# One-core block of attention and mixture of experts: the eight experts over all tokens, or over tokens sorted into tiles by expert

## What is computed

```python
h = _layernorm(x) * (1 + ca) + sa
x = x + ga * attention(h)
h = _layernorm(x) * (1 + cb) + sb
logits = h @ router_w.T
top_w, top_idx = top_k(softmax(logits), 2)
top_w = softmax(top_w)
combine = sum(one_hot(top_idx, 8) * top_w[..., None], axis=1)
hid = silu(einsum('td,efd->tef', h, w1))
y = einsum('tef,edf->ted', hid, w2) * expert_scale
x = x + gb * einsum('te,ted->td', combine, y)
```

## Time and profile before

| | us |
|---|---|
| median of three runs | 678.83 (677.87 to 681.55) |
| the profiled execution, its own time | 677.55 |
| its span, first to last instruction | 675.4 |
| TensorE busy in the span | 586.8 |
| VectorE busy | 541.4 |
| ScalarE busy | 478.3 |
| GpSimd busy | 88.0 |

### The profile page before, as it was taken

One profiled execution on the slowest core, in us unless ns is written; L12 is line 12 of the kernel. 1 busy time (PEld: TensorE's weight loads), 2 busy tenths in 40 slices (PEclk: granted clock), 3 DMA queues, 4 the chain that ended last, 5 costly groups with the idle time before them and its releaser, 6 DMA issues. The chain is left out here.

```text
span 675.4 us, 14685 instructions
## 1 busy us (share of the span) xinstructions
PE 586.8 (87%) x5838; PEld 318.4 (47%) x5838; DVE 541.4 (80%) x840; ACT 478.3 (71%) x925; POOL 88.0 (13%) x166
## 2 busy tenths in 40 slices
PE   4556588979988899899999898996899999999996
PEld 3312132432433433334324333553687778787784
DVE  4797699989898889898998998455567888777775
...
DMA packets 34200, 30.40 MB, mean 45 GB/s; under 512 B 2956, under 2 KB 32332, under 8 KB 33868
## 3 DMA queue, kind: packets, MB, share of 16 engines
q1 hardware_dynamic: 33824, 29.10, 17.6%
...
q10 hardware_dynamic: 312, 0.41, 0.2%
...
## 5 line engine op out<-in xcount | busy, mean ns | idle before, releaser
L1098 ACT ACTIVATE probs<-b 128x512 f32<-128x512 f32 (+1 forms) x576 | 298.7, 570 | 94.6 <-PE b L638 44.6
L866 DVE TENSOR_REDUCE part<-b 128x2 f32<-128x1024 f32 (+2 forms) x320 | 328.1, 1061 | 39.4 <-PE b L553 18.0
L606 PE MATMUL pv<-probs,v_cur 128*32 128x256 f32 (+1 forms) x2432 | 177.7, 376 | 0.0
L638 PE MATMUL b<-aug 55*128 55x512 bf16 (+3 forms) x640 | 115.0, 357 | 44.7 <-ACT probs L1098 30.5
L578 PE MATMUL b<-aug 52*128 52x512 bf16 (+3 forms) x640 | 116.8, 363 | 17.7 <-DVE part L866 14.6
L1125 ACT ACTIVATE probs<-b 128x512 f32<-128x512 f32 x128 | 81.2, 634 | 46.6 <-PE b L736 46.4
L988 DVE TENSOR_TENSOR hs_lo<-probs,hs_hi 128x512 fp32r<-128x512 f32 x128 | 86.6, 696 | 29.1 <-ACT hs_hi L1125 28.5
L638 PEld LDWEIGHTS b<-aug 55*128 55x128 bf16 x640 | 36.8, 93 | 154.7 <-ACT probs L1098 136.5
L606 PEld LDWEIGHTS pv<-probs,v_cur 128*32 128x32 f32 x2432 | 51.7, 110 | 74.9 <-issue 46.8
L1125 ACT ACTIVATE hs_hi<-b 128x512 fp32r<-128x512 f32 x128 | 82.2, 642 | 0.0
L734 PE MATMUL b<-h_hi,w_hi 128*128 128x512 f32 (+1 forms) x128 | 52.2, 408 | 1.1 <-DVE hs_lo L988 1.0
...
## 6 DMA issues: line engine op xcount, KB each, us to landing
yn<-comb_scratch SPq DMA_DIRECT2D x32, 256.0 KB, 5.2
aug<-q_scratch SPq DMA_DIRECT2D x6, 384.0 KB
aug<-k_scratch SPq DMA_DIRECT2D x6, 384.0 KB
w1T_sb<-in_w1T SPq DMA_DIRECT2D x1, 2048.0 KB, 8.8
w2T_sb<-in_w2T SPq DMA_DIRECT2D x1, 2048.0 KB, 13.3
q_scratch<-pieces SPq DMA_DIRECT2D x4, 384.0 KB, 2.8
k_scratch<-pieces SPq DMA_DIRECT2D x4, 384.0 KB, 3.3
x_sb<-in_x SPq DMA_DIRECT2D x4, 256.0 KB, 5.8
```

Source lines behind the costliest of these rows:

```text
L606: return mm(pv[32 * hh:32 * hh + 32, c0:c1], v_cur[:, kb, hh, :], probs[:, step_ % 2, hh, at_:at_ + c1 - c0], start=(kb == 0 and c0 == 0), ...
L638: done.append(mm(pair[half][:, at_:at_ + w], k_aug[g % 2][n, b, kb * P:kb * P + P], q_aug[g % 2][n, b, (j + 1) * CW - w:(j + 1) * CW], sta ...
L866: ins = nc.vector.tensor_reduce(dst, b1[:, slot:slot + 2, at_:at_ + w], AX.X, ALU.max)
L1098: nc.scalar.activation(probs[:, p % 2, hh, 0:w], b2[:, (n2 - 1) % RING2, 0:w], ACT.Exp).then_inc(exp_done, 1)
```

## The change

The split into high and low parts is dropped; the expert stage works in plain fp32. Tokens are handled in two halves of 1024. For each half the ranks of its 2048 (token, choice) pairs within their expert are counted by matmuls with a lower triangle (count), and place on VectorE turns them into row numbers and gives each of 23 tiles its expert (an expert begins at a new tile; 16 full ones and 7 for the rounding). GpSimd sends every pair's normalised row of 128 features, with its return row and its weight (ROW = 130), to its place in DRAM by 16 indirect DMAs of 128 rows (send). Unused rows hold targets in a spare region, which blank and two DMAs write in group 0. Then 46 tiles follow, with DEEP = 4 buffers: SyncE reads the tile's expert into a register and loads w1 of it and the 128 rows; VectorE copies w2 of it (stage); TensorE turns, multiplies up and down; ScalarE adds the modulation and takes silu; VectorE weights and gates (keep); GpSimd scatters the 128 results to DRAM (return_tile). SyncE loads the results of each chunk, two rows per token, and VectorE adds them to x (join).

The last chunk's project, turn, logits and routing run beside tiles 3 to 17, its sends before the result of tile 17. In the attention, the first three groups' values are normalised in the next group: the row of sums of each head goes to DRAM, comes back spread over 128 partitions for one reciprocal, and again by way of DRAM, spread over the rows, to GpSimd's multiplication (scale_values). Only the fourth group keeps norm. The tables for the late parts are three to five steps earlier. w1T is no longer held in SBUF.

```diff
+SUMS_OUT, SUMS_IN, INVERT, INVERSE_OUT, INVERSE_IN = 6, 8, 9, 11, 13
+SCALE_AT = [15, 16, 17, 18]
+BLANK_AT = [5, 10, 13]
+NORM_AT = {17: [0, 1], 22: [2]}
+PROJECT = {19: 0, 21: 1, 26: 2}
+RESIDUAL = {20: 0, 22: 1, 27: 2}
+TURN = {22: 0, 24: 1, 29: 2}
+LOGITS = {23: 0, 25: 1, 31: 2}
+DOUBLE = {22: 0, 24: 1, 29: 2}
+ROUTE = {26: 0, 28: 1, 29: 2, 31: 3}
+ROUTE_EXP = {28: 0, 30: 1}
+COUNT_AT = 30
+PLACE_AT = 32
+HALFN = NT // 2
+ROW = C + 2
+NTILE = HALFN * TOPK + E - 1
+TILES = 2 * NTILE
+DEEP = 4
+LATE_PROJECT, LATE_RESIDUAL, LATE_TURN, LATE_LOGITS = 3, 4, 7, 9
+LATE_ROUTE = {10: 0, 12: 1, 13: 2, 15: 3}
+LATE_EXP = {11: 0, 14: 1}
+LATE_COUNT, LATE_PLACE, LATE_SCATTER = 14, 16, 17
+JOIN_AT = {NTILE + 7: 0, NTILE + 9: 1}
...
+                    if g and p == SUMS_OUT:
+                        sp.wait_ge(yT_s, NC_ * g)
+                        for h in range(HG):
+                            sp.dma_start(sums_dram[h:h + 1, :], yn[32 * h + D:32 * h + D + 1, (g - 1) * T:g * T]).then_inc(sums_out, 16)
+                    if g and p == SUMS_IN:
+                        sp.wait_ge(sums_out, 16 * HG * g)
+                        sp.dma_start(sums[:, :], sums_dram.rearrange("h (p t) -> (h p) t", t=T // 32)).then_inc(sums_in, 16)
+                    if g and p == INVERSE_OUT:
+                        sp.wait_ge(invert_s, g)
+                        sp.dma_start(inverse_dram.rearrange("h (p t) -> (h p) t", t=T // 32), sums[:, :]).then_inc(inverse_out, 16)
+                    if g and p == INVERSE_IN:
+                        sp.wait_ge(inverse_out, 16 * g)
+                        if g > 1:
+                            sp.wait_ge(yn_s, NC_ * (g - 1))
+                        for h in range(HG):
+                            sp.dma_start(inverse[32 * h:32 * h + D + 1, :], inverse_dram[h:h + 1, :].to_broadcast([D + 1, T])).then_inc(inverse_in, 16)
...
+            def load_tile(j):
+                k, half = j % DEEP, j // NTILE
+                if j % NTILE == 0:
+                    sp.wait_ge(place_s, half + 1)
+                e = sp.value_load(expert[0:1, half, j % NTILE:j % NTILE + 1], min_val=0, max_val=E - 1)
+                if j >= DEEP:
+                    sp.wait_ge(up_ps, j - DEEP + 1)
+                sp.dma_start(w1s[:, k, :], a["w1T"][:, ds(e * F, F)]).then_inc(w1s_in[k], 16)
+                if j % NTILE == 0:
+                    sp.wait_ge(sent_in, 16 * TOPK * HALFN * (half + 1))
+                if j >= DEEP:
+                    sp.wait_ge(y_out[k], 16 * (j // DEEP))
+                sp.dma_start(xt[:, k, :], slot_dram[j * P:(j + 1) * P, :]).then_inc(xt_in[k], 16)
+            def load_results(c):
+                for k, n in tile_outs(NTILE * (c // 2 + 1)):
+                    sp.wait_ge(y_out[k], n)
+                src = y_dram[c * CW * TOPK:(c + 1) * CW * TOPK, :].rearrange("(n p k) c -> p n k c", p=P, k=TOPK)
+                if c >= 2:
+                    sp.wait_ge(joined, c - 1)
+                sp.dma_start(yfin[:, c % 2, :, :, :], src).then_inc(y_in[c % 2], 16)
...
+            for j in range(TILES):
+                load_tile(j)
+                if j in JOIN_AT:
+                    load_results(JOIN_AT[j])
+            for c in range(2):
+                store_output(c)
+            for c in range(2, NC_):
+                load_results(c)
+            for c in range(2, NC_):
+                store_output(c)
...
+            def count(k):
+                pe.wait_ge(both_s, k + 1)
+                out = b1[:, 3, :] if k == 0 else b2[:, 2, :]
+                n0 = HALFN * k
+                mm(out[:, 0:HALFN * E], lower[:, :], both[:, n0:n0 + HALFN, :], start=True, stop=False, skip_group_check=True)
+                for i in range(HALFN):
+                    later = [P, HALFN - i, E]
+                    last = mm(out[:, (i + 1) * E:(HALFN + 1) * E], full[:, :], both[:, n0 + i:n0 + i + 1, :].to_broadcast(later),
+                              start=False, stop=(i == HALFN - 1), skip_group_check=True)
+                last.then_inc(count_ps, 1)
...
+            def turn_tile(j):
+                k = j % DEEP
+                pe.wait_ge(xt_in[k], 16 * (j // DEEP + 1))
+                if j >= 2:
+                    pe.wait_ge(tT_s, j - 1)
+                nc.tensor.transpose(b2[:, j % 2, 0:P], xt[:, k, 0:C], ident[:, :]).then_inc(tT_ps, 1)
+            def up(j):
+                k = j % DEEP
+                pe.wait_ge(w1s_in[k], 16 * (j // DEEP + 1))
+                pe.wait_ge(tT_s, j + 1)
+                if j >= 2:
+                    pe.wait_ge(silu_s, j - 1)
+                for f in range(FC):
+                    last = mm(b1[:, j % 2, f * P:(f + 1) * P], w1s[:, k, f * P:(f + 1) * P], hTt[:, j % 2, :], start=True, stop=True)
+                last.then_inc(up_ps, 1)
+            def down(j):
+                k = j % DEEP
+                pe.wait_ge(w2s_s, j + 1)
+                pe.wait_ge(silu_s, j + 1)
+                if j >= 2:
+                    pe.wait_ge(yt_s, j - 1)
+                for f in range(FC):
+                    last = mm(b1[:, 2 + j % 2, 0:C], hst[:, j % 2, f, :], w2s[:, k, f, :], start=(f == 0), stop=(f == FC - 1))
+                last.then_inc(down_ps, 1)
...
+            pe.wait_ge(place_s, 1)
+            turn_tile(0)
+            for j in range(TILES):
+                if j + 1 < TILES:
+                    turn_tile(j + 1)
+                up(j)
+                if j:
+                    down(j - 1)
+                if j == LATE_PROJECT:
+                    for i in range(TPC):
+                        project(NC_ - 1, i)
+                if j == LATE_TURN:
+                    turn_late(NC_ - 1)
+                if j == LATE_LOGITS:
+                    logits(NC_ - 1)
+                if j == LATE_COUNT:
+                    count(1)
+            down(TILES - 1)
...
+            def place(k):
+                n = slice(HALFN * k, HALFN * (k + 1))
+                wide, square, each = [P, HALFN, E], [P, E, E], [P, NTILE, E]
+                counts = b1[:, 3, :] if k == 0 else b2[:, 2, :]
+                dve.wait_ge(count_ps, k + 1)
+                dve.wait_ge(tables_s, 1)
+                of, to = tiles_of[:, k, :], tiles_to[:, k, :]
...
+                step(V.tensor_reduce(spot_f[:, :, :], spot[:, :, :, :], AX.X, ALU.add))
+                V.tensor_copy(spots[:, :, n], spot_f[:, :, :]).then_inc(place_s, 1)
...
+            def stage(j):
+                half = j // NTILE
+                if j % NTILE == 0:
+                    dve.wait_ge(place_s, half + 1)
+                    dve.wait_ge(late_in, 5 * 16)
+                e = dve.value_load(expert[0:1, half, j % NTILE:j % NTILE + 1], min_val=0, max_val=E - 1)
+                if j >= DEEP:
+                    dve.wait_ge(down_ps, j - DEEP + 1)
+                V.tensor_copy(w2s[:, j % DEEP, :, :], w2T[:, ds(e * FC, FC), :]).then_inc(w2s_s, 1)
+            def keep(j):
+                k = j % DEEP
+                dve.wait_ge(down_ps, j + 1)
+                if j >= DEEP:
+                    dve.wait_ge(y_out[k], 16 * (j // DEEP))
+                V.scalar_tensor_tensor(yt[:, k, :], b1[:, 2 + j % 2, 0:C], xt[:, k, C + 1:C + 2], gate[:, 1, :], ALU.mult, ALU.mult).then_inc(yt_s, 1)
+            def join(c):
+                dve.wait_ge(y_in[c % 2], 16 * (c // 2 + 1))
+                xc = x_sb[:, TPC * c:TPC * (c + 1), :]
+                step(V.tensor_tensor(xc, xc, yfin[:, c % 2, :, 0, :], ALU.add))
+                V.tensor_tensor(xc, xc, yfin[:, c % 2, :, 1, :], ALU.add).then_inc(joined, 1)
+            for j in range(DEEP - 1):
+                stage(j)
+            for j in range(TILES):
+                if j:
+                    keep(j - 1)
+                if j + DEEP - 1 < TILES:
+                    stage(j + DEEP - 1)
+                if j == LATE_RESIDUAL:
+                    residual(NC_ - 1)
+                if j == LATE_LOGITS + 1:
+                    keep_logits(NC_ - 1)
+                if j in LATE_ROUTE:
+                    route(1, LATE_ROUTE[j])
+                if j == LATE_PLACE:
+                    place(1)
+                if j in JOIN_AT:
+                    join(JOIN_AT[j])
+            keep(TILES - 1)
...
+            def tile_features(j):
+                act.wait_ge(tT_ps, j + 1)
+                if j >= 2:
+                    act.wait_ge(up_ps, j - 1)
+                nc.scalar.activation(hTt[:, j % 2, :], b2[:, j % 2, 0:P], ACT.Identity, bias=modc[:, 2:3], scale=modc[:, 3:4]).then_inc(tT_s, 1)
+            def silu(j):
+                act.wait_ge(up_ps, j + 1)
+                if j >= 2:
+                    act.wait_ge(down_ps, j - 1)
+                nc.scalar.activation(hst[:, j % 2, :, :].rearrange("p f t -> p (f t)"), b1[:, j % 2, :], ACT.Silu).then_inc(silu_s, 1)
+            tile_features(0)
+            for j in range(TILES):
+                if j + 1 < TILES:
+                    tile_features(j + 1)
+                silu(j)
+                if j == LATE_TURN:
```

(29 more changed lines are left out.)

400 lines of the change are left out of this document (145 added, 255 removed).

## The result

| | before | after |
|---|---|---|
| median of the runs, us | 678.83 (677.87 to 681.55) | 714.88 (712.69 to 721.7) |
| profiled execution, its own time | 677.55 | 721.7 |
| its span | 675.4 | 719.9 |
| ratio to before | | 1.0525, interval 1.049 to 1.0561 |

The change makes the kernel 5.3% slower. The forecast was 734 us, with a range of 662 to 790. The profiled execution of after is the longest of its five (the others have spans of 710 to 713 us).

The account below looks back on a forecast made before the run. TensorE's work was taken to bound the dense expert stage before. After: tile 4's rows at 499.9 us, 41 tiles at 4.70 to 692.6, then 16.9, 2, 5.1 and 14.8 give 731.4, time 734 us, +8%; range 662 to 790.

Parts of the forecast that it names:

- The loop: Tile stage: four row buffers cover only two tiles' round trip through scatter and reload; 4.70 us a tile for 41 tiles.
- X(j+2) to D(j): From tile j+2's rows reaching SBUF to the end of tile j's down product: 2.33 us at full clock.
- R: Time per tile in the tile stage, half of one round: 4.19 us at full clock, 5.22 at half, 4.70 taken.
- The start: First tile's rows in SBUF at 490.6 us, after placement at 468.5, 16 scatters of 17.6, landing 2.3 and load 2.2.
- The stall before tile 17: Before tile 17's result, placement and the second half's 16 scatters, 17.6 us on GpSimd, hold the tiles: +16.9 us.
- Late work on the engines: Last chunk's project, turn, logits and count on TensorE beside the tiles: about 9 us, most in idle time; +2 us.
- L: From a tile's finished down product to its buffer's reloaded rows: keep, scatter issue, landing, reaction and load; 6.05 us.
- 1, the clock at one level: TensorE's clock stays at one level in the tile stage: 713 us at full, 755 at half; chance 0.20.
- 2, a short scatter path: In the tile stage, scatter issue takes 0.41 us and landings 1.8: time 655 us; chance 0.22.
- 3, a slow GpSimd: In the tile stage, scatter issue takes 1.8 us, landings 3.3 and 3.1: about 815 us; chance 0.08.
- 4, VectorE's copy locks GpSimd out: In the tile stage, VectorE's copies of w2 keep GpSimd from its work: 758 us; chance 0.13.
- 5, the loop doesn't bind: In the tile stage, results land early, so TensorE's 2.3 us a tile hold: 633 us; chance 0.05.

Follow-up runs that it names:

- rows5: The changed kernel with five row and result buffers instead of four, weight buffers still four: 669.54 us, ratio 0.9855 to before.
- rows8: The changed kernel with eight row and result buffers instead of four, weight buffers still four: 645.14 us, ratio 0.9496 to before.
- now1: The changed kernel with the w1 load of tiles 4 on cut to 8 of 512 columns, leaving out part of the computation: 703.81 us, ratio 1.0341.
- early: rows8 with last chunk's project, turn and residual before tile 0, routing beside tiles 1 to 6, sends in twos ahead of results 7 to 14: 652.88 us.
- warm: The changed kernel with five unread 128x128 matmuls on TensorE before each tile's turn from tile 18 on: 718.75 us, ratio 1.0574.
- oldnorm: The changed kernel with all groups' norms back in the last group on VectorE, no way over DRAM: 719.55 us, ratio 1.0592.
- delay: The changed kernel with a fill of 1024 columns on GpSimd ahead of each tile's scatter: 740.71 us, ratio 1.0883.

## Why the prediction was right, and which sizes were off

**The mechanism is the one forecast.** "TensorE's idle before the tiles' transposes ended by DMA xt" is the L778 row with 96.0 us; the four buffers that cover two tiles are shown by rows5 and rows8, where nothing but the number of buffers differs. The gap before tile 0, the gap after tile 16 and the stages at a mixed clock are there. The sign is as forecast.

Three of the signs that the forecast named came out otherwise. TensorE was busy for 69% and 66% of the two stretches of tiles, not for about half. The mean pitch is 3.99, below the 4.2 to 5.2 (in turn longer and shorter, as in 4.7, 2.4, 4.5, 2.7 from result 21 on). And attention's end, which was to prove the forecast wrong if it moved by over 5 us, lay 6.0 us later than before and 7.6 later than the 478 forecast. That last one is not the change's: TensorE's last product of the attention began at 479.1 in the trace of before and at 485.2 in after's, but at 474.7 to 480.6 in those of the other kernels (now1 apart, at 490.0, with two of the late releases described under early ahead of it).

**The loop, 4.70 forecast, 3.99 measured.** This term was mis-sized most. Per round of two tiles, in us:

| step of the forecast | forecast | measured |
|---|---|---|
| X(j+2) to D(j): 2.33 at full clock, 4.39 at half, the mean of both | 3.36 | 2.63 |
| keep and its hand-over to GpSimd | 0.35 | 0.63 |
| issue, landing, SyncE's reaction: 1.1 + 2.3 + 0.1 | 3.50 | 2.89 |
| load of the rows | 2.20 | 1.91 |
| sum | 9.41 | 8.05 |

Over the 41 tiles that the forecast charges with it, this is 0.71 x 41 = 29 us. Of the 1.36 a round, 0.73 are in the first row. The clock does alternate, as in these rows of after's TensorE timeline, in which eight records (four matmuls) take 1.92 us against 1.06 at full clock, ten us earlier in the same timeline:

```profile
672.12 0.48 PE L778 MATMUL b<-ident_sb,xt 128*128 128x128 f32 x1 [0.70 <-DMA xt<-slot_scratch]
672.39 1.92 PE L787 MATMUL b<-hTt,aug 128*128 128x128 f32 x8
674.09 1.92 PE L797 MATMUL b<-aug,hst 128*128 128x128 f32 x8
```

But the granted clock of the stretch is 0.85, which is seven tenths of the time at the upper of the two levels (0.7 x 1 + 0.3 x 0.5), not half of it. With the forecast's own 2.33 and 4.39 that share gives 2.95, so 0.41 of the 0.73 are the clock's; the other 0.32 are the steps, which take 2.16 at a clock of 1.00 (warm). Of the rest, 0.61 are the scatter: the forecast added GpSimd's 1.1 us to a landing of 2.3 taken from SyncE's DMAs. All the scatters of after, and those DMAs of the tiles in its last stretch (median us from issue to landing):

```profile
L1354 POOL DMA_INDIRECT y_scratch<-yt,xt x46: 953/956/1120, 511.4 to 708.2; - x46
...
DMA to landing us min/median/max: 2.2/2.6/4.6
```

```profile
aug<-in_w1T SPq DMA_DIRECT2D x24, 256.0 KB, 2.8
xt<-slot_scratch SPq DMA_DIRECT2D x24, 65.0 KB, 1.8
...
y_scratch<-yt,xt POOLq DMA_INDIRECT x26, 2.5
```

2.5 us are from the start of GpSimd's instruction to the landing, its 0.96 included, so 1.5 lie behind it. The row taken for the load (32 KB in 1.8) was right and the value chosen between rows, 2.2, was high. The Trainium skill (DMA: Bandwidth & Descriptors, Anatomy of one DMA) puts a fixed 2.0 us and the bytes at 436 KB per us on a DMA of GpSimd, an estimate of 2.15 us for 64 KB; the forecast named it and kept it out of the sum. The shortest scatter here, 2.2 us, agrees, and the median of 2.6 is 0.4 above it. As for R, that sentence's 3.57 at full clock stands beside 3.43 for the round shown at full clock, where the sum's own was 4.19.

**The start, 490.6 forecast, 503.3 measured.** Sends began at 479.4 against 468.5. This is the step of the forecast that fell: place(0) was taken to be ready four us after 464, and attention to end at 478. In the profiled execution attention ended at 485.6, of which 3.2 us were lost by 74 us and 3.3 more between 141 and 165; the clock there is 0.74 and 0.86 (0 to 74, 74 to 165 us), against 0.80 and 0.93 before. In the profiled executions of the eight other kernels, whose attention part is that of after except in oldnorm, sends began at 469.6 to 475.5. So 4 to 10 of the 11 us belong to this execution, and the rest is place(0) itself, late by 1 to 7 us: it stands on VectorE behind routing part 3, which waits for the logits. The sends took 20.2 us (16 x 1.27) instead of 17.6, since the 0.30 us between two of them had not been counted; landing and load took 3.7 instead of 4.5.

**The stall before tile 17, +16.9 forecast:** 21.5 less a pitch of 4.2 is 17.3. In it the sends had been taken 2.6 us too short, and place(1), counted at 4 us ahead of keep(16), was over before them (results 15 and 16 stand 4.2 us apart, as others do). **Late work on the engines, +2:** results 0 to 16 have a pitch of 4.23, 0.24 more than the later ones, so 3.8 us. The first four tiles took 12.5 us where 9.3 were forecast. **From the last transpose to the end, 5.1 + 14.8 = 19.9:** 19.3.

So in the profiled execution: 12.7 later at the start, and tiles that took 197.3 us instead of the forecast's 220.9 (45 tiles, the stall included), 0.6 less at the end: 731.4 + 12.7 - 23.6 - 0.6 = 719.9. The forecast was nearer to this execution than its steps were to theirs: by luck the late start hid half of the loop's error. Against the median of 714.88 it is 19 us high, and the median lies at the lower end, 715, of the forecast's own range. (That range was drawn a little narrow: 1 us in L is 20.5 us over 41 tiles, so it should have read some 713 to 755.)

**The rivals.** 1, the clock at one level: neither; with the second half's tiles at full clock (warm) the time doesn't fall. 2, a short scatter path: halfway true in the landings, false in the issue, 0.96 us and not 0.41; its point of no change, an issue of 0.6 and L of 4.95, was not reached: L is 0.63 + 2.89 + 1.91 = 5.43. 3, a slow GpSimd: false; delay, which makes it one, gives 740.71. 4, VectorE's copy locks GpSimd out: 46 copies of 0.43 us ran, in the second half one beside each scatter of tiles 20 to 41, begun 0.13 to 0.15 us after it (664.70 and 664.84 above). No scatter of a result took over 1.12 us, and eight of these 22 landed in 2.22 to 2.26, as soon as any without a copy beside it (2.22 to 2.48). The Trainium skill (SBUF — State Buffer, SBUF: two separate sides) says that GpSimd can't write descriptors during such a copy; no cost of that shows here, at this share of copies. 5, the loop doesn't bind: false in after and true in rows8, which reaches 645 us where the rival had 633.

**Why half the work is slower.** TensorE's product of the sparse form needs 1.9 us a tile (rows8), 87 us for 46 tiles, 104 less than the dense stage's 191.5. In after, the ring gives back (4.0 - 1.9) x 45 = 94 of them; the two queues of sends cost 17.7 + 17.3, the tail of scatter, loads and stores 15.0 more than before, and attention ended 6 later in the profiled execution: -104 + 94 + 35 + 15 + 6 = 46, against the 44.5 that the spans differ by.
